# Cross-attention and a quantised feed-forward on one core: scores ahead of the up product in each tile's first slot

## The chip, the cores and the metric

The kernel runs on one core of a Trainium2 chip. A core has five engines with an instruction queue each, which run in order and meet only at semaphores: TensorE (PE in the profile; its weight loads stand apart as PEld), VectorE (DVE), ScalarE (ACT), GpSimd (POOL) and SyncE (SP), which issues nearly all DMA transfers. The metric is the device time of one execution in microseconds (us).

## The reference, cut to what matters

The input is 8 batches of 512 rows with 512 columns; the context has 120 rows per batch. A block of cross-attention with 16 heads of 32 columns is added to the input, then a feed-forward block whose weights are ternary and whose activations are rounded to 8 bits.

```python
def proj(x, w, bias): ...                       # 16 heads of 32
Q = proj(layernorm(x), wq, bq); K = proj(ctx, wk, bk); V = proj(ctx, wv, bv)
scores = jnp.einsum('bhqd,bhkd->bhqk', Q, K) / jnp.sqrt(32)
scores = jnp.where(mask == 0, 1e-09, scores)
attn = jax.nn.softmax(scores, axis=-1)
x = x + (attn @ V) @ wo + bo
...
# bitlinear(x, w, b) = act_quant(rmsnorm(x)) @ weight_quant(w).T + b
h = gelu(bitlinear(layernorm(x), w1, b1))       # 512 -> 2048
x = x + bitlinear(h, w2, b2)                    # 2048 -> 512
```

## The kernel before, in words

The rows are cut into 32 tiles of 128, four to a batch. Every tile passes through a software pipeline written out by hand: time is cut into 128 slots, four to a tile, and for each engine a function `slot(n)` lists, in program order, what that engine does in slot n. Different stages of several tiles stand in one slot. Nothing reorders the lists at run time, so what stands ahead of an instruction on its engine delays it.

What the slots hold, as far as it matters here:

- A softmax group is four of a tile's 16 heads, one group per slot. In a tile's first slot (n divisible by 4) `scores(k)` on PE computes the scores of all 16 heads: 16 products into the four PSUM banks `ps_s`, one bank per group. It waits until the exponentials of all four groups of the tile before have been read from these banks (`exp_done` at 4k; the last of them is group n-1).
- DVE masks and takes the maximum of group n in slot n (`softmax_max`, L831 and L834). ACT does the exponentials of group n-1 in slot n (`exps`, L693, four pairs of instructions), and then copies the transposed probabilities of group n-3 out of `ps_t` (L665). POOL scales the probabilities (L1114), PE transposes them (`turn_probs`, L466).
- From slot 14 on, each slot has one quarter of the up product of another tile: `ffn_up` on PE, four matmuls into the bank `ps_z` (L507), and `evac_up` on DVE, which copies and scales it into `hid` (L873). There is one `ps_z` bank, so `ffn_up` of slot n waits for `evac_up` of slot n-1 (`z_evac`).
- DVE's own order in a tile's first slot is fixed: `evac_down` (L892) and `oT_low` (L799) of other tiles, then `evac_up` (L873), then `softmax_max` (L831). In the other three slots `softmax_max` stands ahead of `evac_up`.
- ACT's GELU for a tile (L700) follows in the slot after its last up quarter, behind a table load; another table load stands ahead of the next exponentials.
- In a tile's fourth slot PE does attention times V (L478), in its second the output projection (L405). Projections and transposes for the next batch lie in between, in a pattern of 16 slots per batch (L405 with `wq`, L435, L412).

Slots 0, 4, 8 and 12 of a batch's 16 are first slots of a tile. Behind the up product and the scores, slots 0 and 4 go on with a transpose of the next batch's rows (L412), slots 8 and 12 with a q projection (L405). In the last batch, slots 112 to 127, there is neither.

Of the kernel before, what the change touches and what calls it, by code (L numbers as in the profile page):

```python
# [27 lines left out]
def xattn_bitffn_kernel(nc, x, ctx_in, mask, wq, bq, wk, bk, wv, bv, wo, bo, w1, b1, w2, b2, out):  # L28
# [5 lines left out]
    G = D // P  # L34
# [47 lines left out]
    def tile_at(n, first):  # L82
        k, r = divmod(n - first, FC)
        return k if r == 0 and 0 <= k < NT else None
# [42 lines left out]
    with ExitStack() as stack:  # L127
# [93 lines left out]
        def wait(eng, name, count):  # L221
            if count > 0:
                eng.wait_ge(s[name], count)
# [142 lines left out]
        def _(pe):  # L366
            def wait_free(use):

                kind, a, k = use
                if kind == "x":  # L370
                    wait(pe, "xT_low", KD * a + k + 1)
                elif kind == "k":
                    wait(pe, "keyT_ready", a + 1)
                elif kind == "c":
                    wait(pe, "turn_evac", YT_ACT[use] + 1)
                elif kind == "m":
                    wait(pe, "wT_dve", 2 * a + k // 2 + 1)
                else:
                    wait(pe, "y_evac", a + 1)
# [28 lines left out]
            def turn_xn(a, k):  # L408
                bank = turn_free(("x", a, k))
                wait(pe, "xn_ready", T * (a + 1))  # L410
                for t in range(T):
                    last = nc.tensor.transpose(bank[:, t * P:(t + 1) * P], xn[:, t, k * P:(k + 1) * P], ident[:])  # L412
                last.then_inc(s["turn_full"], 1)
# [17 lines left out]
            def project_ctx(a, what, w):  # L431
                bank = a_bank((what, a, 0))
                wait(pe, "turn_evac", YT_ACT[("c", a, 0)] + 1)
                for k in range(KD):
                    last = nc.tensor.matmul(bank[0:S2, :], ctxT[:, k], w[:, k], start=(k == 0), stop=(k == KD - 1))  # L435
                last.then_inc(s["a_full"], 1)

            def project_q(a, g):
                bank = a_bank(("q", a, g))
                if g == 0:  # L440
                    wait(pe, "xT_low", KD * (a + 1))
                for k in range(KD):
                    wh, wl = wq_h[:, k, g * P:(g + 1) * P], wq_l[:, k, g * P:(g + 1) * P]
                    last = product3(bank[:], k, ((wh, xnT_h[:, k]), (wh, xnT_l[:, k]), (wl, xnT_h[:, k])))
                last.then_inc(s["a_full"], 1)

            def scores(k):
                a = k // T
                wait(pe, "keyT_ready", a + 1)
                if k % T == 0:  # L450
                    wait(pe, "a_evac", AJ_ACT[("q", a, G - 1)] + 1)
                wait(pe, "exp_done", G * k)
                for g in range(G):
                    for i in range(HG):
                        rows = slice(i * HD, (i + 1) * HD)
                        last = nc.tensor.matmul(ps_s[i][:, g * S2:(g + 1) * S2], qT[rows, k % QR, g],  # L456
                                                keyT[rows, a % 2, g], start=True, stop=True)
                last.then_inc(s["sc_full"], 1)

            def turn_probs(n):  # L460
                if n == 0:
                    wait_free(YT[FIRST - 2])
                wait(pe, "p_evac", n)
                wait(pe, "prob_ready", n + 1)
                for g in range(G):
                    last = nc.tensor.transpose(ps_t[0:S2, g * P:(g + 1) * P], prob[:, n % 3, g * S2:(g + 1) * S2],  # L466
                                               ident[:])
                last.then_inc(s["p_full"], 1)

            def attend(k):  # L470
                a = k // T
                bank = a_bank(("o", k, 0))
                wait(pe, "v_ready", a + 1)
                wait(pe, "p_evac", G * k + HG)
                for g in range(G):
                    for i in range(HG):
                        h = g * HG + i
                        last = nc.tensor.matmul(bank[i * HD:(i + 1) * HD, g * P:(g + 1) * P],  # L478
                                                v_s[:, a % 2, h * HD:(h + 1) * HD], probT[0:S2, i, g],
                                                start=True, stop=True)  # L480
                last.then_inc(s["a_full"], 1)
# [10 lines left out]
            def ffn_up(k, c):  # L492
                j = FC * k + c
                if j == 0:
                    pe.wait_ge(s["wT_act"], 16)
                    pe.wait_ge(s["wT_dve"], 8)
                if j <= Z0:
                    wait(pe, "z_evac", j)
                else:
                    wait(pe, "z_evac", j - 2)  # L500
                    if j <= Z0 + 2:
                        pe.wait_ge(s["exp_done"], NU)
                if c == 0:
                    wait(pe, f"qxT{k % 3}_in", 16 * (k // 3 + 1))
                bank = z_bank(j)
                for i in range(KD):
                    last = nc.tensor.matmul(bank[:], q_xT[:, k % 3, i], w1T[:, i, c * CH:(c + 1) * CH],  # L507
                                            start=(i == 0), stop=(i == KD - 1))
                last.then_inc(s["z_full"], 1)
# [16 lines left out]
            def total_weights(m):  # L526
                pe.wait_ge(s["abs_act"], 2 * (m + 1))
                pe.wait_ge(s["abs_dve"], 2 * (m + 1))
                wait(pe, "wT_act", 8 * m)
                nc.tensor.matmul(ps_z[:, 0:4], ones, w_abs[:, m], start=True, stop=True).then_inc(s["w_sum"], 1)  # L530

            def turn_piece(j, quarters):
                p = TURN[j]
                if j % 2 == 0:
                    pe.wait_ge(s["w_ready_dve"], j // 2 + 1)
                else:
                    pe.wait_ge(s["w_ready_pool"], j // 2 + 1)
                for q in quarters:
                    if q % 2 == 0:
                        wait(pe, "wT_act", 2 * j + q // 2)  # L540
                        bank = ps_z
                    else:
                        wait_free(Y[Y_N[("m", j, q)] - 1])
                        bank = ps_y
                    for c in range(4):
                        col = c * D + q * P if p < 4 else (4 * q + c) * P
                        last = nc.tensor.transpose(bank[:, c * P:(c + 1) * P], piece_buf[p][:, col:col + P], ident[:])
                    last.then_inc(s["wT_full"], 1)

            def slot(n):  # L550
                if n >= LAG:
                    turn_probs(n - LAG)
                k = tile_at(n, ATT0)
                if k is not None:
                    attend(k)
                if n in TOTAL_AT:
                    total_weights(TOTAL_AT[n])
                if n in TURN_AT:
                    turn_piece(TURN_AT.index(n), (0, 1))
                if n >= UP0:  # L560
                    ffn_up((n - UP0) // FC, (n - UP0) % FC)
                if n % G == 0:
                    scores(n // G)
                if n in PROJ:
                    kind, b, g = PROJ[n]
                    if kind == "q":
                        project_q(b, g)
                    else:
                        if kind == "v" and b == 0:
                            pe.wait_ge(s["wv_in"], 16)  # L570
                        project_ctx(b, kind, wk_s if kind == "k" else wv_s)
                k = tile_at(n, WO0)
                if k is not None:
                    project_out(k)
                if n in TURN_AT:
                    turn_piece(TURN_AT.index(n), (2, 3))
                if n in TURNS:
                    kind, b, k = TURNS[n]
                    if kind == "x":
                        turn_xn(b, k)  # L580
                    elif kind == "c":
                        turn_ctx(b)
                    else:
                        turn_keys(b)
                for half in range(2):
                    k = tile_at(n, DOWN0 + half)
                    if k is not None:
                        ffn_down(k, half)
# [656 lines left out]
```

## Time and profile before

| | us |
|---|---|
| median of 3 runs | 743.72 |
| lowest and highest run | 740.01, 750.9 |
| profiled execution, time | 741.57 |
| its span, first to last instruction | 739.8 |

| engine | busy, share of the span |
|---|---|
| PE | 90% |
| DVE | 82% |
| ACT | 71% |
| POOL | 68% |

The span of the profiled execution is 1.8 us shorter than its time. A batch in the steady part takes about 78.6 us, 19.6 us per tile; two batches with their 32 slots lie between 298.6 and 456.1 us. A row of the timeline gives start, duration, engine, line, operation and tiles, and in square brackets the idle time of that engine just before it with what ended it, where there was any. The ends of matmuls are modelled, so that neighbouring matmuls seem to overlap; starts are the better measure.

### The profile page before, as it was taken

Reading aid. Unit: us, or ns where it says so; the run is one execution under the profiler, and the core shown is the slowest. Engines: PE = TensorE matmul, PEld = TensorE weight load, DVE = VectorE, ACT = ScalarE, POOL = GpSimd, SP = SyncE. Lnnn points to the kernel's source line nnn. Section 1 sums busy time; section 2 is a strip of 40 time slices with the busy share of each in tenths; the row PEclk is TensorE's granted clock in tenths of the full one; section 3 lists DMA queues with packets and bytes.
Section 4 is the critical chain, followed back from the end, with each engine's and each line's share of the span. In section 5 each row is a group of like instructions: output and inputs, shape, how many; then the busy total and the mean of one; then the engine's idle time right before and its main releaser. Section 6 shows DMA issues by size and latency. Waiting matters only on the chain.

```text
span 739.8 us, 13877 instructions
## 1 busy us (share of the span) xinstructions
PE 662.3 (90%) x4856; PEld 428.5 (58%) x4856; DVE 603.0 (82%) x1060; ACT 522.6 (71%) x1455; POOL 506.1 (68%) x645
## 2 busy tenths in 40 slices
PE   8755778989999999999999999999999998888885
PEld 6524566755666567656666666656665664554532
DVE  3397586689979898899888988989798888888783
ACT  2264536686888877886788678868888778887360
POOL 3036363766877787777977687768777668877764
PEclk9977979999999999999999999999999999999997
DMA  9943003034122433343334322351222333333244
GB/s 304 379 151 129 1 15 106 17 55 109 44 63 66 122 78 79 66 122 78 79 65 99 100 65 64 64 116 48 67 65 65 79 65 65 65 65 66 57 79 113
DMA packets 109204, 65.37 MB, mean 88 GB/s; under 512 B 90775, under 2 KB 90775, under 8 KB 108495
## 3 DMA queue, kind: packets, MB, share of 16 engines
q1 hardware_dynamic: 108079, 64.49, 34.9%
q8 instruction: 39, 0.64, 0.3%
q14 instruction: 30, 0.25, 0.1%
q10 hardware_dynamic: 1056, 0.00, 0.1%
HBM read 35.12 MB, written 8.39 MB: 59 GB/s over the span
## 4 chain that ended last, share of the span: by engine, by line
PE 39%; DVE 30%; ACT 11%; issue 7%; POOL 5%; DMA 5%; SPq 3%; DVEq 0%; POOLq 0%; ACTq 0%
PE ps_a L405 13%; PE ps_z L507 6%; PE ps_y L522 5%; PE ps_a L435 4%; DVE hs L880 4%; DVE yw L857 3%; DMA q_xT<-q_x 3%; DVE hid L873 3%; PE ps_a L478 3%; ACT prob L693 3%; PE ps_t L466 2%; POOL hid L1121 2%; POOL q_h L1128 2%; DVE yq L860 2%; DVE bn L817 2%
## 5 line engine op out<-in xcount | busy, mean ns | idle before, releaser
L1114 POOL TENSOR_TENSOR prob<-prob,pinv 128x480 f32<-128x480 f32 x128 | 126.5, 988 | 166.5 <-DVE pinv L839 166.4
L693 ACT ACTIVATE prob<-ps_s,nmax 128x120 f32<-128x120 f32 x512 | 180.5, 384 | 25.2 <-DVE nmax L834 24.9
L507 PE MATMUL ps_z<-w1T,q_xT 128*128 128x512 bf16 x476 | 123.1, 381 | 5.6 <-DMA q_xT<-q_x 5.5
L693 ACT ACTIVATION_READ_ACCUMULATOR prob<-ps_s,nmax 128x1 f32 x512 | 117.4, 229 | 0.0
L522 PE MATMUL ps_y<-w2T,q_hT 128*128 128x512 bf16 x480 | 113.2, 379 | 0.3 <-DMA q_hT<-xn 0.3
L873 DVE SCALAR_TENSOR_TENSOR hid<-ps_z,y_deq,b_row 128x512 f32<-128x512 f32 x119 | 88.6, 745 | 25.2 <-PE ps_z L507 25.1
L831 DVE COPY_PREDICATED_SCALAR ps_s<-hidden_key,masked_c 128x480 f32 x128 | 89.6, 700 | 18.0 <-PE ps_s L456 18.0
L466 PE MATMUL ps_t<-ident,prob 128*120 128x128 f32 x512 | 79.0, 277 | 12.8 <-ACT probT L665 10.2
L834 DVE TENSOR_REDUCE nmax<-ps_s 128x4 f32<-128x480 f32 x128 | 84.2, 658 | 4.4
L665 ACT COPY probT<-ps_t 120x512 f32<-120x512 f32 x128 | 79.5, 621 | 8.7 <-PE ps_t L466 8.6
L522 PEld LDWEIGHTS ps_y<-w2T,q_hT 128*128 128x128 bf16 x480 | 45.9, 98 | 61.1 <-issue 10.4
L466 PEld LDWEIGHTS ps_t<-ident,prob 128*120 128x120 f32 x512 | 60.1, 139 | 33.9 <-ACT probT L665 19.7
L672 ACT ACTIVATE qT<-ps_a,bq_col 128x512 f32<-128x512 f32 (+1 forms) x32 | 19.7, 616 | 75.6 <-PE ps_a L405 70.9
L880 DVE TENSOR_REDUCE hs<-hid 128x1 f32<-128x2048 f32 x32 | 72.8, 2276 | 0.0
L1121 POOL TENSOR_SCALAR hid<-hid,hs 128x2048 f32<-128x2048 f32 x31 | 61.1, 1972 | 13.5 <-DVE hs L886 7.1
L700 ACT ACTIVATE hid<-hid 128x2048 f32<-128x2048 f32 x32 | 61.2, 1913 | 11.3 <-DVE hid L873 11.0
L507 PEld LDWEIGHTS ps_z<-w1T,q_xT 128*128 128x128 bf16 x476 | 43.5, 98 | 43.5 <-issue 13.5
L1128 POOL TENSOR_SCALAR q_h<-hid 128x2048 bf16<-128x2048 f32 x30 | 58.0, 1933 | 2.6
L405 PE MATMUL ps_a<-xnT_h,wq_h 128*128 128x512 f32 x124 | 52.7, 425 | 7.8 <-DVE oT_l L799 3.9
L405 PE MATMUL ps_a<-wo_h,oT_h 128*128 128x512 f32 x128 | 56.9, 444 | 2.4 <-DVE oT_l L799 1.5
L708 ACT ACTIVATE q_h<-hid 128x2048 bf16<-128x2048 f32 x28 | 54.3, 1938 | 0.0
L405 PE MATMUL ps_a<-wo_l,oT_h 128*128 128x512 f32 x128 | 50.9, 398 | 0.0
(155 smaller groups left out, 1400.8 us busy)
## 6 DMA issues: line engine op xcount, KB each, us to landing
xn<-in_x_dram SPq DMA_DIRECT2D x8, 1024.0 KB, 5.8
x<-in_x_dram SPq DMA_DIRECT2D x32, 256.0 KB, 2.7
out_dram<-x SPq DMA_DIRECT2D x32, 256.0 KB, 3.4
hid<-in_L_ffn_w_dram SPq DMA_DIRECT2D x4, 1024.0 KB, 8.9
w2T<-in_L_ffn_w_dram SPq DMA_DIRECT2D x2, 1024.0 KB, 14.0
ctx_k<-in_ctx_dram SPq DMA_DIRECT2D x8, 240.0 KB, 3.7
ctx_k<-in_mask_Bx1xSxS_ik_dram SPq DMA_DIRECT2D x7, 240.0 KB, 2.9
wk_s<-in_L_xattn_wk_dram SPq DMA_DIRECT2D x1, 1024.0 KB, 8.8
```

The lines of the kernel that those rows point to most:

```text
L405: last = nc.tensor.matmul(bank, w, m, start=(k == 0 and i == 0), stop=(k == KD - 1 and i == 2))
L466: last = nc.tensor.transpose(ps_t[0:S2, g * P:(g + 1) * P], prob[:, n % 3, g * S2:(g + 1) * S2], ident[:])
L507: last = nc.tensor.matmul(bank[:], q_xT[:, k % 3, i], w1T[:, i, c * CH:(c + 1) * CH], start=(i == 0), stop=(i == KD - 1))
L522: last = nc.tensor.matmul(y_bank(k)[:], q_hT[:, k % 2, f], w2T[:, f], start=(f == 0), stop=(f == KF - 1))
L665: nc.scalar.copy(probT[0:S2, i], ps_t[0:S2, :].rearrange("p (g q) -> p g q", g=G)).then_inc(s["p_evac"], 1)
L693: last = nc.scalar.activation(prob[:, n % 3, g * S2:(g + 1) * S2], ps_s[n % HG][:, g * S2:(g + 1) * S2], ACT.Exp, bias=nmax[:, n % 4, g:g ...
L831: v.copy_predicated(sc, hidden_key[:, k // T % 2, k % T].unsqueeze(1).to_broadcast([P, G, S2]), masked_c[:].unsqueeze(2).to_broadcast([P, ...
L834: v.tensor_reduce(out=nmax[:, n % 4], in_=sc, op=ALU.max, axis=AX_X, negate=True).then_inc(s["sc_max"], 1)
L873: v.scalar_tensor_tensor(hid[:, k % 2, c * CH:(c + 1) * CH], z_bank(FC * k + c)[:], y_deq[:, k % 8:k % 8 + 1], b1_row[:, c * CH:(c + 1) * ...
L880: v.tensor_reduce(out=hs[:, 3, t:t + 1], in_=hid[:, k % 2], op=ALU.max, axis=AX_X, apply_absolute_value=True).then_inc(s["h_abs"], 1)
L1114: gp.tensor_tensor(pr, pr, pinv[:, n % 4].unsqueeze(2).to_broadcast([P, HG, S2]), ALU.mult).then_inc(s["prob_ready"], 1)
L1121: gp.tensor_scalar(hid[:, k % 2], hid[:, k % 2], hs[:, 5, t:t + 1], MAGIC, ALU.mult, ALU.add).then_inc(s["h_magic"], 1)
```

## The change: what it does, and the diff

In the list of PE, `scores` moves from behind `ffn_up` to ahead of it. Since scores are only in slots with n divisible by 4, only these slots change, and of them only those from slot 16 on, where there is an up product. No instruction is added or removed, and the lists of the other engines and their waits are as before.

```diff
                 if n in TURN_AT:
                     turn_piece(TURN_AT.index(n), (0, 1))
+                if n % G == 0:
+                    scores(n // G)
                 if n >= UP0:
                     ffn_up((n - UP0) // FC, (n - UP0) % FC)
-                if n % G == 0:
-                    scores(n // G)
                 if n in PROJ:
```

PE's queue around slot 64, a batch's slot 0. The first two rows are the end of the fourth slot of the tile before, the last row is the head of slot 65. Before the change:

```order
L507 MATMUL ps_z<-w1T,q_xT 128x512 x3
L522 MATMUL ps_y<-w2T,q_hT 128x512 x8
L466 MATMUL ps_t<-ident,prob 120x128 [waits prob_ready,p_evac]
L466 MATMUL ps_t<-ident,prob 120x128 x3
L507 MATMUL ps_z<-w1T,q_xT 128x512 [waits z_evac]
L507 MATMUL ps_z<-w1T,q_xT 128x512 x3
L456 MATMUL ps_s<-keyT,qT 128x120 [waits exp_done,keyT_ready]
L456 MATMUL ps_s<-keyT,qT 128x120 x15
L412 MATMUL ps_y<-ident,xn 128x128 [waits xn_ready,y_evac]
L412 MATMUL ps_y<-ident,xn 128x128 x3
L466 MATMUL ps_t<-ident,prob 120x128 [waits prob_ready,p_evac]
```

The same place with the change:

```order
L507 MATMUL ps_z<-w1T,q_xT 128x512 x3
L522 MATMUL ps_y<-w2T,q_hT 128x512 x8
L466 MATMUL ps_t<-ident,prob 120x128 [waits prob_ready,p_evac]
L466 MATMUL ps_t<-ident,prob 120x128 x3
L456 MATMUL ps_s<-keyT,qT 128x120 [waits exp_done,keyT_ready]
L456 MATMUL ps_s<-keyT,qT 128x120 x15
L507 MATMUL ps_z<-w1T,q_xT 128x512 [waits z_evac]
L507 MATMUL ps_z<-w1T,q_xT 128x512 x3
L412 MATMUL ps_y<-ident,xn 128x128 [waits xn_ready,y_evac]
L412 MATMUL ps_y<-ident,xn 128x128 x3
L466 MATMUL ps_t<-ident,prob 120x128 [waits prob_ready,p_evac]
```

The wait for `exp_done` now stands ahead of the up product's four matmuls.

DVE's queue in the same slot, equal before and with the change:

```order
L839 RECIPROCAL pinv<-psums 128x4 [waits exp_done]
L892 SCALAR_TENSOR_TENSOR x<-ps_y,h_deq,x 128x512 [waits y_full,hdeq_ready,x2b2_ready]
L799 TENSOR_TENSOR oT_l<-ps_a,oT_h 128x512 [waits a_evac]
L873 SCALAR_TENSOR_TENSOR hid<-ps_z,y_deq,b_row 128x512 [waits z_full]
L831 COPY_PREDICATED ps_s<-hidden_key,masked_c 128x480 [waits sc_full]
L834 TENSOR_REDUCE nmax<-ps_s 128x4 [waits sc_masked]
L839 RECIPROCAL pinv<-psums 128x4 [waits exp_done]
L831 COPY_PREDICATED ps_s<-hidden_key,masked_c 128x480 [waits sc_full]
```

Nothing moved here: L873, the copy of the up product, stands ahead of L831, the first reader of the scores.

## Rows read from the trace of the kernel before

**Rows 1.** The page, part 1: engine, busy us (share of the span) xinstructions.
```profile
PE 662.3 (90%) x4856; PEld 428.5 (58%) x4856; DVE 603.0 (82%) x1060; ACT 522.6 (71%) x1455; POOL 506.1 (68%) x645
```

**Rows 2.** Windows: busy us (instructions) of PE, PEld, DVE, ACT, POOL, then clock, DMA.
```profile
155.00:165.00 10.00, 7.91 (x61) 5.32 (x60) 8.43 (x16) 6.86 (x31) 9.27 (x12) 0.83 0.48 60
377.45:456.05 78.60, 76.75 (x585) 49.86 (x584) 69.29 (x128) 63.77 (x179) 60.74 (x80) 1.00 0.35 81
612.00:668.00 56.00, 46.24 (x417) 28.44 (x418) 50.08 (x92) 45.18 (x135) 45.47 (x58) 1.00 0.37 66
```

**Rows 3.** Timeline, slot 64: PE.
```profile
376.80 0.65 PE L466 MATMUL ps_t<-ident,prob 128*120 128x128 f32 x4 [0.21 <-ACT probT L665]
377.28 1.03 PE L507 MATMUL ps_z<-w1T,q_xT 128*128 128x512 bf16 x4
378.27 1.17 PE L456 MATMUL ps_s<-keyT,qT 32*128 32x120 f32 x32
379.37 0.66 PE L412 MATMUL ps_y<-ident,xn 128*128 128x128 f32 x4
```

**Rows 4.** Timeline, slot 64: ACT, a copy, and the last exponentials of the tile before.
```profile
376.07 0.67 ACT L665 COPY probT<-ps_t 120x512 f32<-120x512 f32 x1
...
377.81 0.31 ACT L693 ACTIVATION_READ_ACCUMULATOR prob<-ps_s,nmax 128x1 f32 x1
```

**Rows 5.** Timeline, slot 64: DVE.
```profile
379.17 0.74 DVE L873 SCALAR_TENSOR_TENSOR hid<-ps_z,y_deq,b_row 128x512 f32<-128x512 f32 x1
379.82 0.71 DVE L831 COPY_PREDICATED_SCALAR ps_s<-hidden_key,masked_c 128x480 f32 x1
```

**Rows 6.** Timeline, slot 67: PE's up product and DVE's copy of it.
```profile
392.79 1.04 PE L507 MATMUL ps_z<-w1T,q_xT 128*128 128x512 bf16 x4
393.86 0.75 DVE L873 SCALAR_TENSOR_TENSOR hid<-ps_z,y_deq,b_row 128x512 f32<-128x512 f32 x1 [0.81 <-PE ps_z L507]
```

**Rows 7.** Waits of ACT from 381.3 to 396.8: total us, times, longest.
```profile
ACT prob L693 <- DVE nmax L834: 0.6, 1, 0.6
```

**Rows 8.** Timeline, slot 68: ACT's last exponentials and DVE's copy.
```profile
395.99 0.30 ACT L693 ACTIVATION_READ_ACCUMULATOR prob<-ps_s,nmax 128x1 f32 x1
397.52 0.74 DVE L873 SCALAR_TENSOR_TENSOR hid<-ps_z,y_deq,b_row 128x512 f32<-128x512 f32 x1
```

**Rows 9.** Timeline, slot 72: ACT, PE and DVE.
```profile
414.11 0.23 ACT L693 ACTIVATION_READ_ACCUMULATOR prob<-ps_s,nmax 128x1 f32 x1
414.35 0.60 PE L466 MATMUL ps_t<-ident,prob 128*120 128x128 f32 x4
417.86 0.74 DVE L873 SCALAR_TENSOR_TENSOR hid<-ps_z,y_deq,b_row 128x512 f32<-128x512 f32 x1
```

**Rows 10.** Timeline, slot 20: ACT, PE and DVE.
```profile
158.99 0.30 ACT L693 ACTIVATION_READ_ACCUMULATOR prob<-ps_s,nmax 128x1 f32 x1
157.97 0.65 PE L466 MATMUL ps_t<-ident,prob 128*120 128x128 f32 x4 [2.09 <-ACT probT L665]
159.91 2.08 PE L456 MATMUL ps_s<-keyT,qT 32*128 32x120 f32 x32
162.05 0.72 DVE L831 COPY_PREDICATED_SCALAR ps_s<-hidden_key,masked_c 128x480 f32 x1 [1.29 <-PE ps_s L456]
```

**Rows 11.** Timeline, slot 108: ACT and PE.
```profile
592.85 0.31 ACT L693 ACTIVATION_READ_ACCUMULATOR prob<-ps_s,nmax 128x1 f32 x1
594.60 0.50 PE L405 MATMUL ps_a<-xnT_h,wq_h 128*128 128x512 f32 x1
```

**Rows 12.** Timeline, slot 112: ACT and DVE.
```profile
612.91 0.31 ACT L693 ACTIVATION_READ_ACCUMULATOR prob<-ps_s,nmax 128x1 f32 x1
614.28 0.74 DVE L873 SCALAR_TENSOR_TENSOR hid<-ps_z,y_deq,b_row 128x512 f32<-128x512 f32 x1
```

**Rows 13.** Timeline, slot 124: ACT and DVE.
```profile
664.96 0.29 ACT L693 ACTIVATION_READ_ACCUMULATOR prob<-ps_s,nmax 128x1 f32 x1
666.85 0.74 DVE L873 SCALAR_TENSOR_TENSOR hid<-ps_z,y_deq,b_row 128x512 f32<-128x512 f32 x1
```

## Prediction

> **What bounds the kernel now.** I read the page's part 1 first: PE is busy 90% of the span, DVE 82%, ACT 71% [rows 1]. That names no engine that is always the limit. The windows say more: in the batch from 377.45 to 456.05 us PE is idle for 78.60 - 76.75 = 1.85 us only, at full clock, and in the last batch for 56.00 - 46.24 = 9.76 us, also at full clock [rows 2]. So the steady part has hardly any room on PE, but the question is which wait ends last around the moved product, and that is read from the timeline of slot 64 on three engines.
>
> On PE the up product starts at 377.28, the scores at 378.27, the next step at 379.37 [rows 3]. So the up product takes 0.99 us there and the scores 1.10, from start to start. The scores need `exp_done` of the group before. On ACT that is the last accumulator read, which ends at 377.81 + 0.31 = 378.12 [rows 4]: 0.84 us after the start of the up product, and 0.15 us before the scores start. The reader is to see that the up product now fills exactly the time in which ACT finishes. PE does not wait for `exp_done` because it has this other work first. On DVE the copy of the up product starts at 379.17, after DVE's other work and without idle time before it, and the mask on the scores follows at 379.82 [rows 5]. The up product was ready about a microsecond earlier, so DVE, not PE, sets the pace here.
>
> **The change, part by part.** Nothing is added or removed; 16 score products and 4 up matmuls change places in the 28 first slots from 16 to 124. The list of PE now has the wait for `exp_done` ahead of both. Queued behind it on PE are the up product and all that follows; DVE waits for the up product with the scores' own reader behind that; ACT waits for DVE's maximum. The DMA queue is not moved past anything: SP waits for DVE and POOL results that precede the copy.
>
> *The new path in a slot.* From the end of ACT's last read to DVE's copy there are three steps. ACT's end to PE's start: ACT's copy ends at 376.07 + 0.67 = 376.74 and PE starts at 376.80, 0.06 [rows 3, 4]. The scores: 1.10. The up product up to DVE's start, where DVE was waiting for it: 393.86 - 392.79 = 1.07 [rows 6]. Together 2.23 us.
>
> *Slot 64* (a batch's slot 0): 378.12 + 2.23 = 380.35 against 379.17 [rows 5], so DVE is 1.18 us late. Who carries it on? The mask and maximum come right behind the copy, and the next exponentials on ACT already waited 0.6 us for that maximum, which is ACT's only wait from 381.3 to 396.8 us [rows 7]. ACT therefore starts 1.18 us late and works without a break up to the last exponentials of the tile. It has nothing in which the delay could be lost, although DVE has: it waits 0.81 us for PE at 393.86 [rows 6].
>
> *Slot 68* (slot 4): ACT's last read ends at 395.99 + 0.30 = 396.29, plus 2.23 is 398.52 against 397.52 [rows 8]: another 1.00 us, on top of the 1.18 that ACT brings along. PE comes earlier than ACT in both.
>
> *Slots 72 and 76* (8 and 12): no loss. In slot 72 ACT is done at 414.34, before PE's transposes that start at 414.35. The scores could start 0.48 us behind those (376.80 to 377.28 in [rows 3]), at 414.83, and 1.10 + 1.07 later DVE could copy, at 417.00, but it comes only at 417.86 [rows 9]. Slot 76 reads the same with less to spare. No gain either: DVE takes the up product first, so scores that are ready a microsecond sooner are read by nobody.
>
> So a batch loses 1.18 + 1.00 = 2.18 us. Five batches read like this (slots 32 to 107): 10.9 us. Around them:
>
> - Slot 16 reads like slot 68: 1.0.
> - Slot 20: PE has been idle 2.09 us before its transposes, and the scores take 2.08 us instead of 1.17; the mask waits 1.29 us for them [rows 3, 10]. The mean clock from 155 to 165 us is 0.83 [rows 2], so PE spends about a third of that at the lower of its two levels (1.2 GHz) and the rest at 2.4. ACT is done at 158.99 + 0.30 = 159.29; scores at 159.35, up product at 161.43 if still slow, copy at 162.50 at full clock and 163.57 at the lower one, mask 0.65 later [rows 5], against 162.05 [rows 10]: 1.1 to 2.2 late. I take 1.3, near the lower end, since the third of 10 us is over by about then.
> - Slot 108: ACT's end at 593.16, plus 0.06 and 1.10 and the 0.99 of the up product gives 595.31 for the projection, which started at 594.60 [rows 11]: 0.7.
> - The last batch, four slots: 613.22 + 2.23 against 614.28 is 1.17 [rows 12], 665.25 + 2.23 against 666.85 is 0.63 [rows 13]; four times their mean, 0.9, is 3.6.
>
> Sum: 1.0 + 1.3 + 10.9 + 0.7 + 3.6 = 17.5 us. The profiled execution took 741.57 us, so 759.1; that execution lies 2.2 us below the median of 743.72, from which it would be 761.2. I forecast **760**. Bounds: nothing at the least, if every added wait falls into idle time; at the most 1.18 in all 28 slots, 33 us, which slots 72 and 76 exclude. The own range of this sum is 13 to 21 us.
>
> *The clock.* The row shows that PE's clock was low after the 2.09 us of idle time [rows 10], and high in the last batch with 9.76 us of idle time spread over it [rows 2]. The change puts some 0.7 us of new idle time (376.80 + 0.48 to 378.18) ahead of the scores in each losing slot. The Trainium skill (TensorE: Matmul & The Clock Gate, Part 1) says that the slow clock is the default that an idle engine falls back to, and its closing table warns of idle gaps between bursts of matmuls. By that rule this change could cost more than its waits; by the rows at full clock the sum stands as it is. The trace agrees with the rule at slot 20 and does not show it in the last batch.
>
> **Rivals.**
>
> *The waits swallow it* (not slower). If ACT does not carry the delay, because its order leaves it time that the rows don't show, only PE's own delay remains: 0.06 + 1.10 + 0.99 after 378.12 is 380.27 against 379.37, 0.90 us a slot, 1.8 for the two of a batch, and PE has 1.85 us of idle time in it [rows 2]. Then the five batches cost nothing and slot 16 neither, and 1.3 + 0.7 + 3.6 = 5.6 us are left: 747. For it speak DVE's 0.81 us; against it that ACT has one wait in 15 us [rows 7]. It decides from the point where ACT has 1.18 us to spare between the maximum of a tile's first group and its last exponentials. Chance 0.18.
>
> *The clock falls too* (slower still). In the last batch, where PE already idles most, each of the four slots would run scores and up product at the lower clock: 2.17 us more each, 8.7 in all, so 768. For it speaks slot 20, against it the clock of 1.00 from 612 to 668 us. Chance 0.13.
>
> *The early scores are worth something* (faster). If DVE's mask did wait for scores in many slots, they would come a microsecond sooner. Only slot 20 shows such a wait, 1.29 us [rows 10], so the gain would be a microsecond or two: 740. Chance 0.04. That the change does nothing is excluded, since PE's printed order does move and PE's queue is in order.
>
> **How the numbers follow.** The sum has 0.62, the rivals 0.18, 0.13 and 0.04, and 0.03 is left for something else. 2% is 14.9 us, about what a measurement of this kernel can tell from no change. Of the sum's 13 to 21 us about four fifths lie above that: 0.50, with the clock's 0.13 and 0.01 of the rest 0.64 for slower; faster by 2% has 0.02; the other 0.34 is within 2%. The range goes from 749 to 767: it has the whole of the sum from either base and the upper part of the first rival and the lower of the second.
>
> **What would show it.** In the changed kernel's slot 64: scores 0.05 to 0.1 us after ACT's last read with PE idle some 0.7 us before them, and DVE's copy waiting for PE where it had no wait; slots of the kinds 0 and 4 with this wait, 8 and 12 without; a batch of about 80.8 us instead of 78.6; ACT's idle time before the first exponentials of a tile longer by the same 1.2. The forecast is wrong if a batch stays at 78.6 us although DVE waits (first rival), or if PE's clock in the last batch is below 1.00 (second).

## The result, and the profile after

| | before | with the change |
|---|---|---|
| median, us | 747.21 (4 runs) | 761.3 (4 runs) |
| lowest and highest run | 740.01, 750.9 | 760.62, 761.52 |
| profiled execution, time and span | 741.57, 739.8 | 760.62, 758.8 |

The ratio of the mean times is 1.0199 with a 95% interval of 1.0109 to 1.0289: slower beyond its interval, though whether by more or by less than 2% stays open. A fourth run of the kernel before, beside the changed one, lifted its median from 743.72 to 747.21; in three later measurements it was 740.65, 743.02 and 740.85. The two profiled executions differ by 19.0 us in span and are compared below. The forecast was 760, with 749 to 767 as its range.

The page of the changed kernel, its parts 1 and 4:

```profile
PE 665.5 (88%) x4856; PEld 428.4 (56%) x4856; DVE 604.2 (80%) x1060; ACT 522.2 (69%) x1455; POOL 505.4 (67%) x645
...
ACT 46%; PE 22%; DVE 19%; issue 9%; DMA 2%; POOL 1%; SPq 0%; ACTq 0%; DVEq 0%; POOLq 0%
```

Busy times are those of before within 3.2 us [rows 1]: the 19 us are nearly all waits. Of the chain that ended last, 46% now lies on ACT, where it was 11%.

The timeline of slot 64, ACT, PE and DVE, in the order of [rows 3 to 5]:

```profile
384.76 0.31 ACT L693 ACTIVATION_READ_ACCUMULATOR prob<-ps_s,nmax 128x1 f32 x1
...
385.21 1.17 PE L456 MATMUL ps_s<-keyT,qT 32*128 32x120 f32 x32 [0.82 <-ACT prob L693]
...
386.31 1.04 PE L507 MATMUL ps_z<-w1T,q_xT 128*128 128x512 bf16 x4
...
387.19 0.60 PE L412 MATMUL ps_y<-ident,xn 128*128 128x128 f32 x4
...
387.39 0.75 DVE L873 SCALAR_TENSOR_TENSOR hid<-ps_z,y_deq,b_row 128x512 f32<-128x512 f32 x1 [1.19 <-PE ps_z L507]
...
388.06 0.71 DVE L831 COPY_PREDICATED_SCALAR ps_s<-hidden_key,masked_c 128x480 f32 x1
```

PE, which had no wait here, now stands idle for 0.82 us and starts at 385.21, 0.14 us after ACT's read ends at 385.07, and DVE stands idle for 1.19 us where it had no wait. From ACT's end to DVE's copy it takes 387.39 - 385.07 = 2.32 us.

The chain of waits in the same place (start, us, what):

```profile
383.69 1.39 ACT prob L693 x8
385.08 0.14 issue
385.21 1.17 PE ps_s L456 x32
386.38 0.98 PE ps_z L507 x4
387.36 0.02 issue
387.39 0.03 DVE hid L873
387.42 0.64 issue
388.06 0.72 DVE ps_s L831
388.78 0.02 issue
388.80 0.67 DVE nmax L834
389.47 0.02 issue
389.50 1.48 ACT prob L693 x8
390.97 0.48 ACT probT L665
391.45 0.02 issue
391.47 1.05 ACT L700
...
402.64 0.49 ACT probT L665
403.13 1.39 ACT prob L693 x8
404.52 0.14 issue
404.65 1.17 PE ps_s L456 x32
```

From 389.50 to 404.52 the chain does not leave ACT, and at its end stands slot 68 with the same pattern again. ACT's wait for the maximum, at the head of that stretch, grew from 0.6 us [rows 7] to 1.1:

```profile
ACT prob L693 <- DVE nmax L834: 1.1, 1, 1.1
```

That growth is less than half of the delay, because another wait now takes up part of the same time, one that the prediction did not name: ACT's list has the copy of PE's transposes (L655) before the exponentials, and these transposes come later too. First before, then with the change:

```profile
380.06 0.59 ACT L655 CAST xnT_h<-ps_y 128x512 fp32r<-128x512 f32 x1 [1.46 <-PE ps_y L412]
```

```profile
387.82 0.58 ACT L655 CAST xnT_h<-ps_y 128x512 fp32r<-128x512 f32 x1 [2.28 <-PE ps_y L412]
```

Together ACT's idle time ahead of the tile's first exponentials grew by (2.28 - 1.46) + (1.1 - 0.6) = 1.3 us, where 1.2 was forecast. The maximum is still the later of the two: the exponentials start at 389.50, right behind it.

The window of the batch that starts with slot 64 (columns as in [rows 2]):

```profile
383.50:464.40 80.90, 77.10 (x584) 49.73 (x584) 70.07 (x128) 63.64 (x179) 60.65 (x80) 1.00 0.34 79
```

The batch takes some 80.9 us instead of 78.6, at full clock.

As the common measure of all kernels I take the start of DVE's mask on a tile's first group (L831). From slot 28 to slot 104 it takes 372.68 us before and 384.34 with the change: 11.66 more, or **2.33 us a batch** over five batches, each with one slot of kind 0 and one of kind 4. All per-batch numbers below are made like this, against the profiled execution of before. Between these slots the granted clock is 1.00 in the profiled execution of every kernel of this document, so they are free of the clock; spans and medians are not.

### The profile page after: what moved, and what is told of

It is laid out like the page before. It is cut to its first block, busy times and chain, and to the rows that moved or that the text cites. A ratio compares the mean times of both kernels' runs of the same rounds, so it can differ in the third digit from the quotient of the medians.

```text
span 758.8 us, 13877 instructions
## 1 busy us (share of the span) xinstructions
PE 665.5 (88%) x4856; PEld 428.4 (56%) x4856; DVE 604.2 (80%) x1060; ACT 522.2 (69%) x1455; POOL 505.4 (67%) x645
## 4 chain that ended last, share of the span: by engine, by line
ACT 46%; PE 22%; DVE 19%; issue 9%; DMA 2%; POOL 1%; SPq 0%; ACTq 0%; DVEq 0%; POOLq 0%
ACT prob L693 17%; PE ps_a L405 8%; ACT hid L700 6%; ACT q_h L708 5%; ACT probT L665 4%; PE ps_s L456 4%; PE ps_z L507 4%; ACT L693 4%; ACT L700 4%; DVE hs L880 2%; DVE hid L873 2%; DVE yw L857 2%; DVE ps_s L831 2%; DVE nmax L834 2%; PE ps_a L435 1%
## 5 line engine op out<-in xcount | busy, mean ns | idle before, releaser
L693 ACT ACTIVATE prob<-ps_s,nmax 128x120 f32<-128x120 f32 x512 | 180.0, 383 | 34.1 <-DVE nmax L834 33.8
L507 PE MATMUL ps_z<-w1T,q_xT 128*128 128x512 bf16 x476 | 125.4, 387 | 1.7 <-DVE hid L873 1.2
L873 DVE SCALAR_TENSOR_TENSOR hid<-ps_z,y_deq,b_row 128x512 f32<-128x512 f32 x119 | 88.6, 745 | 46.9 <-PE ps_z L507 46.4
L693 ACT ACTIVATION_READ_ACCUMULATOR prob<-ps_s,nmax 128x1 f32 x512 | 117.2, 229 | 0.0
L831 DVE COPY_PREDICATED_SCALAR ps_s<-hidden_key,masked_c 128x480 f32 x128 | 89.5, 699 | 16.2 <-PE ps_s L456 16.2
L665 ACT COPY probT<-ps_t 120x512 f32<-120x512 f32 x128 | 79.2, 619 | 11.1 <-PE ps_t L466 10.9
L700 ACT ACTIVATE hid<-hid 128x2048 f32<-128x2048 f32 x32 | 61.2, 1912 | 11.3 <-DVE hid L873 10.9
L507 PEld LDWEIGHTS ps_z<-w1T,q_xT 128*128 128x128 bf16 x476 | 40.6, 98 | 45.7 <-issue 9.0
L456 PE MATMUL ps_s<-keyT,qT 32*128 32x120 f32 x1024 | 39.5, 292 | 15.7 <-ACT prob L693 14.3
```

Of the source, the lines that this page charges most:

```text
L665: nc.scalar.copy(probT[0:S2, i], ps_t[0:S2, :].rearrange("p (g q) -> p g q", g=G)).then_inc(s["p_evac"], 1)
L693: last = nc.scalar.activation(prob[:, n % 3, g * S2:(g + 1) * S2], ps_s[n % HG][:, g * S2:(g + 1) * S2], ACT.Exp, bias=nmax[:, n % 4, g:g ...
L700: nc.scalar.activation(hid[:, k % 2], hid[:, k % 2], ACT.Gelu).then_inc(s["gelu_done"], 1)
L831: v.copy_predicated(sc, hidden_key[:, k // T % 2, k % T].unsqueeze(1).to_broadcast([P, G, S2]), masked_c[:].unsqueeze(2).to_broadcast([P, ...
L873: v.scalar_tensor_tensor(hid[:, k % 2, c * CH:(c + 1) * CH], z_bank(FC * k + c)[:], y_deq[:, k % 8:k % 8 + 1], b1_row[:, c * CH:(c + 1) * ...
```

## The experiments

**Only slots 8 and 12, and only slots 0 and 4.** The change is cut in two.

```diff
-                if n % G == 0:
+                if n % G == 0 and n % U in (8, 12):    # the other: (0, 4)
                     scores(n // G)
                 if n >= UP0:
                     ffn_up((n - UP0) // FC, (n - UP0) % FC)
+                if n % G == 0 and n % U not in (8, 12):
+                    scores(n // G)
```

> Scores ahead of the up product only in slots 8 and 12 of each batch's 16 (24, 28, ... 108, 120, 124); in slots 0 and 4 behind it as before. Theory (cost only where ACT's last exponentials end later than PE could start the scores): nothing up to slot 104, 0.3 to 0.7 us at 108, about 1.1 at 120 and 0.7 at 124, so 2 to 3 us above the kernel before, 742 of span. Rival (any scores ahead of the up product push DVE's copy back by their 1.1 us): 14 x 1.1 = 15 us, as much as the other half of the slots.

> The complement: scores ahead only in slots 0 and 4 of a batch (16, 20, 32, 36, ... 112, 116). Theory: nearly the whole loss, 16 us: 1.1 at slot 16, 2.0 at 20, five times 2.3, 1.2 and 1.1 in the last batch; span about 756. Rival (each first slot pays alike): about 10 us.

Measured: slots 8 and 12 alone 745.66 us, ratio 1.0053 (1.0015 to 1.0091), span 742.1, and -0.06 us a batch; slots 0 and 4 alone 759.3 us, ratio 1.0212 (1.0139 to 1.0286), span 752.6, and 2.34 us a batch. The halves are as different as the rows of ACT's end said: where ACT is done before PE gets there, scores ahead of the up product cost nothing. What the first half loses lies elsewhere: 1.5 us ahead of slot 12, where the kernels are alike, and 2.5 in the last batch, of which 1.4 were made up at the end. The second span is 3.4 us below what I expected, with the loss of the batches in full. Slot 20 added only 0.2 us in that execution, and the clock says why: PE had stood idle for 2.08 us ahead of its transposes as before, but the clock stayed at 1.00 from 158 to 166 us. It is also the lowest of that kernel's four executions; by the medians this half loses 18.7 us.

**The wait without the move.** PE's order is that of before, and the up product waits as well.

```diff
                 if n >= UP0:
+                    if n % G == 0:
+                        wait(pe, "exp_done", n)
                     ffn_up((n - UP0) // FC, (n - UP0) % FC)
```

> PE's order as before (up product, then scores), but the up product of a first slot also waits for exp_done. It parts the two costs: the wait put ahead of the up product, and the 1.1 us of scores put ahead of it. Theory, from the rows of before: the copy can start at 378.12 + 0.06 + 1.07 = 379.25 instead of 379.17, and the mask waits for the scores, 378.12 + 0.06 + 0.99 + 1.10 + 0.04 = 380.31 instead of 379.82, +0.5 in slot 64 and +0.3 in slot 68: 0.8 a batch, about 6 us in all, span 746. Rival (the whole loss is the wait, wherever the scores stand): 2.3 us a batch, span 757 to 759.

Measured: 752.6 us, ratio 1.0138 (1.007 to 1.0207), span 752.0, 1.00 us a batch. Slot 64, ACT, PE and DVE (the wait adds two lines to the source, L695, L875 and L833 are L693, L873 and L831):

```profile
382.24 0.31 ACT L695 ACTIVATION_READ_ACCUMULATOR prob<-ps_s,nmax 128x1 f32 x1
...
382.61 1.04 PE L507 MATMUL ps_z<-w1T,q_xT 128*128 128x512 bf16 x4 [0.73 <-ACT prob L695]
...
383.58 1.17 PE L456 MATMUL ps_s<-keyT,qT 32*128 32x120 f32 x32
...
383.69 0.75 DVE L875 SCALAR_TENSOR_TENSOR hid<-ps_z,y_deq,b_row 128x512 f32<-128x512 f32 x1
...
384.88 0.72 DVE L833 COPY_PREDICATED_SCALAR ps_s<-hidden_key,masked_c 128x480 f32 x1 [0.45 <-PE ps_s L456]
```

The wait is nearly as long as in the change (0.73 us), but the up product comes first behind it and DVE's copy is not idle before it; the mask then waits 0.45 us. So the same wait costs 1.0 us a batch in this order and 2.33 in the other. The span is 6 us above what I expected, and the batches (1.0 instead of 0.8) explain only 1 of it. Outside them 7.2 us were lost where my total left 2: 0.9 ahead of slot 12, where the kernels are alike, 1.5 between slots 12 and 28, 3.4 in the last batch and 1.4 behind it. In the last batch 1.85 us came in slot 120 alone, next to a stretch of low clock (a mean of 0.72 from 650 to 656 us); I did not take the others apart.

**DVE follows PE's order.** On top of the change, DVE's mask and maximum stand ahead of its copy in first slots from 16 on.

```diff
+                if n % G == 0 and n >= UP0:
+                    softmax_max(n)
                 if n >= UP0:
                     evac_up((n - UP0) // FC, (n - UP0) % FC)
                 ...
-                if n % G == 0:
+                if n % G == 0 and n < UP0:
                     softmax_max(n)
```

> PE as in the change, and DVE follows it: in first slots from 16 on the mask and maximum of the scores stand ahead of the copy of the up product. Theory (ACT carries the delay, and only the maximum feeds ACT): in slot 64 the scores are there at 378.18 + 1.10 + 0.04 = 379.32, so the mask starts at 379.32 instead of 379.82 and ACT starts its exponentials 0.5 us earlier than before; the copy comes 1.4 us later and with it the next up product (z_evac), which PE pays with about 1 us where it is not idle. Expected between 733 and 748, near the kernel before, and in any case over 10 us faster than the change. Rival (PE or DVE carries the delay): no better than the change, 757 to 760, since PE waits as long and the copy is later still.

Measured: 751.17 us, ratio 1.0113 (1.0049 to 1.0177), span 749.2, 1.08 us a batch. Faster than the change by 10 us, slower than before, and just outside what I expected. Slot 64, by ACT, PE, DVE:

```profile
381.33 0.31 ACT L693 ACTIVATION_READ_ACCUMULATOR prob<-ps_s,nmax 128x1 f32 x1
...
383.08 0.72 DVE L831 COPY_PREDICATED_SCALAR ps_s<-hidden_key,masked_c 128x480 f32 x1 [0.32 <-PE ps_s L456]
...
383.76 0.60 PE L412 MATMUL ps_y<-ident,xn 128*128 128x128 f32 x4
...
384.39 0.58 ACT L655 CAST xnT_h<-ps_y 128x512 fp32r<-128x512 f32 x1 [2.28 <-PE ps_y L412]
...
384.88 0.37 ACT L693 ACTIVATE prob<-ps_s,nmax 128x120 f32<-128x120 f32 x1
...
385.21 1.04 PE L507 MATMUL ps_z<-w1T,q_xT 128*128 128x512 bf16 x4 [0.42 <-DVE hid L873]
```

The mask does start sooner after ACT's end (1.44 us instead of 1.70 before), but ACT gains nothing by it: its list has the copy of PE's transposes (L655) ahead of the exponentials, and these transposes are late behind scores and up product. I had left that wait out. And the late copy makes PE wait 0.42 us.

**ACT without its table loads.** GELU is replaced by an identity in both kernels; its function is left out.

```diff
-                nc.scalar.activation(hid[:, k % 2], hid[:, k % 2], ACT.Gelu).then_inc(s["gelu_done"], 1)
+                nc.scalar.activation(hid[:, k % 2], hid[:, k % 2], ACT.Identity).then_inc(s["gelu_done"], 1)
```

> The kernel before with the GELU replaced by an identity, which is in the same table as the exponentials: the computation leaves out the GELU's function, and ACT loses its two table loads of 1.28 us per tile. It is the base for the next run. ACT has 2.56 us a tile to spare, but DVE and PE set most of the chain of before: 730 to 740 us.

> The same edit on the changed kernel (GELU left out, no table loads). Theory (the loss is ACT's late exponentials, carried from one first slot to the next by an ACT without slack): with 2.56 us a tile taken out of ACT's chain the exponentials are done before PE needs them, and this run lies within 6 us of the run without loads and scores behind, at most 0.8 us a batch. Rival (the loss is the 1.1 us of scores put ahead of the up product, on PE and DVE, whatever ACT does): 2.3 us a batch and 17 to 19 us in all, as between the two kernels themselves.

Measured: scores behind 733.05 us, ahead 739.98; spans 730.7 and 736.9, 6.2 us apart instead of 19.0; -1.18 and -0.13 us a batch, so 1.05 apart instead of 2.33. With 2.56 us a tile taken out of ACT's chain, more than half of the loss a batch is gone. The two waits of PE for ACT in a batch fell from 1.6 us to 0.5 (windows 383.5 to 464.4 of the change and 376 to 455 of this run):

```profile
PE ps_s L456 <- ACT prob L693: 1.6, 2, 0.8
```

```profile
PE ps_s L456 <- ACT prob L693: 0.5, 2, 0.3
```

They did not go to zero, and the difference is a little over what I allowed (0.8 a batch). How much of the 1.05 that are left still hangs on ACT, these two kernels do not say.

**Ahead, but without the wait.** Two attempts. In the first, the fourth bank's products were computed for the second bank instead, so that the third group's exponentials are enough.

```diff
-                wait(pe, "exp_done", G * k)
+                wait(pe, "exp_done", G * k - 1 if k >= 4 else G * k)
                 for g in range(G):
                     for i in range(HG):
+                        if k >= 4 and i == 3:
+                            i = 1
```

> The changed order without its wait: from slot 16 on the four products meant for the fourth bank are computed for the second bank instead (same count and size, so the fourth group's scores are left out and stay those of an old tile), and the scores then need only the exponentials of the third group, which are long done. Theory: in slot 64 the scores start at 377.28 and the copy can start 1.10 + 1.07 later, at 379.45, against 379.17: 0.3 us; in slot 68 395.82 + 2.17 = 397.99 against 397.52: 0.5. So 0.8 us a batch at most, about 6 us in all, 741 to 747 of span, against 758.8 with the wait. Rival (the order costs, not the wait): above 755.

Measured: 770.68 us, ratio 1.0359 (1.0302 to 1.0415), span 769.1. This looked like a refutation and is a fault of the experiment. PE has no wait for ACT in front of the scores any more, but they take longer:

```profile
389.09 2.05 PE L458 MATMUL ps_s<-keyT,qT 32*128 32x120 f32 x32
```

The four products of one round of the inner loop use four different groups of 32 rows (`rows`) and write four different banks; with two of the four in the same row group, and so in the same bank, 16 products took 2.05 us instead of 1.17 [rows 3], both at full clock. Row group and bank changed together, so this run does not say which of them costs. The wait of 0.8 us was exchanged for 0.9 us of work.

In the second attempt the fourth group's products are left out from slot 16 on (`continue` in place of `i = 1`), in three kernels: ahead without the wait, ahead with it, and behind.

> The run before this kind was spoilt by its substitute: products that shared a row group took 2.05 us instead of 1.17. Now from slot 16 on the fourth group's products are left out (12 scores instead of 16, some 0.83 us), scores stand ahead of the up product, and they need only the third group's exponentials. Theory (the wait is the cost): slot 64 copy at 377.28 + 0.83 + 1.07 = 379.18 against 379.17, slot 68 395.82 + 1.90 = 397.72 against 397.52, so 0 to 0.2 us a batch and 1 to 3 us above the 12 products behind. Rival (the scores' time ahead of the up product costs even without the wait): 0.8 us a slot, above 1.5 a batch, 10 us or more.

> The same 12 products ahead, with the wait for all four groups' exponentials as in the change. Theory: slot 64 378.12 + 0.06 + 0.83 + 1.07 = 380.08 against 379.17, 0.9; slot 68 0.7; 1.65 a batch and 11 to 14 us above the 12 products behind. Rival (the order, not the wait): the same as without the wait.

> The base of the two: 12 products from slot 16 on, behind the up product as in the kernel before. DVE sets the pace in the first slots, so 0.27 us less of PE moves little: 736 to 740 of span.

Measured, in this order: 749.45 us, 762.7 and 745.69, ratios to the kernel before 1.0109 (1.0071 to 1.0146), 1.0268 (1.0142 to 1.0394) and 1.0051 (1.002 to 1.0081). Spans 745.9, 762.0, 744.5. A batch costs 0.62 us ahead without the wait and 2.32 with it. So, with the same work in the same order, the wait alone makes 1.7 of 2.3 us. In both the loss is larger than I expected (0 to 0.2 and 1.65 a batch), and for one reason. I had taken 0.83 us for 12 products, but they take as long as 16, as the row of the kernel with the wait shows,

```profile
387.76 1.16 PE L458 MATMUL ps_s<-keyT,qT 32*128 32x120 f32 x24 [0.82 <-ACT prob L695]
```

and with 1.10 us of scores the rows of before give 0.3 + 0.5 = 0.8 us a batch, as I had worked out for the first attempt. The base with 12 products behind is itself 4.7 us longer than before although it does less (I expected no more than 740 of span). Its trace shows where: 1.4 us came between slots 20 and 24, where the mean clock from 162 to 168 us is 0.67 against 0.98 before; and 2.0 between slots 48 and 52, where an up product waited 0.78 us for a transfer (`q_xT`) that was in time before and one DVE instruction (L857 of before) took 2.09 us instead of 0.98. In the other batches it runs as before, within 0.12 us.

**An attempt at a faster kernel.** From the kernel before, with DVE's residue L799 behind the maximum in slots 0 and 4.

```diff
+                k = tile_at(n, LOW0)
+                if k is not None and n >= U and n % U in (0, 4):
+                    oT_low(k)
```

(and the two places ahead leave it out in these slots.)

> An attempt at a version faster than both: the kernel before, with DVE's residue of the attention output (L799, 0.66 us) behind the maximum in slots 0 and 4 of a batch instead of ahead of the copy. The mask then waits for the scores alone: 379.41 instead of 379.82 in slot 64, so ACT starts 0.4 us earlier; the output projection on PE, which needs this residue, starts at about 381.45 instead of 380.97. If ACT carries the chain, up to 0.4 us for each of 16 slots, 6 us faster, 734; if PE does, up to 6 us slower, 746. I expect 736 to 740.

Measured: 741.95 us against 743.02, ratio 0.9968 (0.9937 to 1.0), span 738.6. A batch got 0.08 us longer. The span is within what I expected, but that is no change that this measurement can tell: no version here beats the kernel before.

## Why the prediction was right, point by point

The forecast, 760, and the mechanism held. Start of the mask, by slot, with the change against before:

| term | forecast, us | measured, us |
|---|---|---|
| slot 16 | 1.0 | 1.1 |
| slot 20 | 1.3 | 2.0 |
| five batches, slots 0 and 4 | 10.9 | 11.7 |
| slots 24 and 28 | 0 | -0.1 |
| slot 108 | 0.7 | 0.3 |
| last batch, four slots | 3.6 | 5.1 |
| sum | 17.5 | 20.0 |

The span differs by 19.0, since the changed kernel's execution was 0.7 us ahead before slot 16, and made up 0.3 us at the end. So it is partly luck that the forecast came so close: the terms were 2.5 us short, and 1.0 of that was hidden in stretches for which the sum has no term (ahead of slot 16 and behind slot 124). By medians the difference is 14.1 us against the four runs of before beside it, and 20.65 against the lowest of the three later medians.

*The new path.* I put 2.23 us from ACT's last read to DVE's copy; it is 2.32. The step that was mis-sized is ACT's end to PE's start: 0.06 us by the row of a copy and the transposes behind it, and 0.14 with the scores. It is not the accumulator read that makes the difference: in the kernel with the wait alone the up product started 0.06 us after such a read (382.24 + 0.31 = 382.55, and 382.61). It goes with the matmuls that wait, and why is not shown. 0.09 in each of ten slots is 0.9, against the 0.8 us that the five batches came out above the forecast. (The 0.7 us of new idle time that I gave for PE does not fit its own bracket, which makes 0.90; it was 0.82.)

*Who carries it.* With the change the chain lies on ACT from the first exponentials of a tile to the last. Shortening ACT's chain takes away 1.3 of 2.33 us a batch. The first rival (the waits swallow it, 747) has failed: DVE's idle time behind slot 64 swallowed nothing, since ACT was late by the same amount. What I left out, ACT's wait for PE's transposes (L655), does no more in slot 64 than take up time in which ACT would have waited for the maximum. But not the whole loss is PE's wait for ACT: with 12 products the order by itself costs 0.62 us a batch.

*Slots 8 and 12* cost nothing up to slot 104, by themselves and within the change. In slot 72, ACT ended at 423.41 + 0.23 = 423.64, ahead of PE's transposes at 423.66:

```profile
423.41 0.23 ACT L693 ACTIVATION_READ_ACCUMULATOR prob<-ps_s,nmax 128x1 f32 x1
```

*Slot 20.* Between my bounds of 1.1 and 2.2 us I chose 1.3, since I took the low clock to be over by the time of the up product. It was not:

```profile
159.81 2.08 PE L456 MATMUL ps_s<-keyT,qT 32*128 32x120 f32 x32 [0.36 <-ACT prob L693]
...
161.82 1.89 PE L507 MATMUL ps_z<-w1T,q_xT 128*128 128x512 bf16 x4
```

The granted clock by windows, before (first) and with the change:

```profile
158.00:160.00 2.00, 2.00 (x12) 0.89 (x12) 1.83 (x6) 1.77 (x9) 2.00 (x2) 0.71 0.00 0
...
162.00:164.00 2.00, 2.00 (x13) 1.61 (x14) 1.91 (x4) 1.08 (x4) 1.64 (x6) 0.94 1.29 57
164.00:166.00 2.00, 2.00 (x11) 1.59 (x10) 1.97 (x4) 1.98 (x8) 1.75 (x4) 1.00 1.11 219
```

```profile
158.00:160.00 2.00, 1.29 (x8) 0.92 (x12) 1.90 (x6) 2.00 (x10) 1.91 (x2) 0.54 0.00 0
...
162.00:164.00 2.00, 2.00 (x7) 1.03 (x6) 0.25 (x1) 0.00 (x0) 1.63 (x5) 0.50 1.13 210
164.00:166.00 2.00, 2.00 (x12) 1.61 (x11) 1.97 (x5) 0.73 (x2) 0.26 (x2) 0.75 0.95 80
```

From 160 to 162 us both have 0.50. A window of 2 us at a mean of 0.54 holds 2 x (1 - 0.54) / 0.5 = 1.8 us at the lower level, 1.2 GHz; added up, that is 3.4 us before and 6.8 with the change, where PE had been idle another 0.36 us for ACT. The up product took 1.89 us there instead of 1.04. That the change made the clock stay low is not shown: in the kernel with 12 products behind, whose order is that of before, it was low for 6.8 us too (0.79 from 158 to 160 us, 0.50 from 160 to 166), and with scores ahead in slots 0 and 4 alone it did not fall.

*The clock rival* (768) came true in part, and the sign that I had set for it, a clock below 1.00 in the last batch, did appear. It cost far less than the rival's 8.7 us, since up to slot 124 the clock fell once and not at all four slots. It fell after PE had been idle for 2.90 us:

```profile
659.11 0.65 PE L466 MATMUL ps_t<-ident,prob 128*120 128x128 f32 x4 [2.90 <-ACT probT L665]
659.69 1.77 PE L478 MATMUL ps_a<-probT,v_s 120*32 120x128 f32 x32
661.39 1.89 PE L507 MATMUL ps_z<-w1T,q_xT 128*128 128x512 bf16 x4
```

The window from 658 to 664 us has a mean clock of 0.72, the six windows from 640 to 654 have 1.00; and 650 to 668 of before had idle times of up to 1.6 us in front of the same transposes, at full clock. Slot 120, which follows, lost 1.84 us, where the other three slots of that batch lost 1.1 on average. The Trainium skill (TensorE: Matmul & The Clock Gate, Part 1 and closing table) warns of idle gaps between bursts of matmuls. The trace agrees with that at 659.11, but not every such gap did it: PE had stood idle for 2.77 us ahead of its transposes at 640.63 and for 2.94 us ahead of those at 678.30, and the clock stayed at 1.00. Nor is it shown that the change brought the fall: two kernels with the scores behind had one there as well, with a mean of 0.72 from 662 to 668 us (12 products behind) and of 0.57 from 660 to 664 (L799 behind the maximum). Behind slot 127 it fell once more (0.72 from 696 to 702 us, after 2.82 us of idle time), but in the last 33 us of the change its mean was 0.95, and 0.84 in the last 34 of before; there the two executions differ the other way.

The sum is 20.0 where 17.5 was forecast: 0.8 for the latency, 0.7 for slot 20, 1.5 in the last batch (by my estimate some 0.8 of it the clock, 1.84 less 1.1, and 0.4 the latency), less 0.4 at slot 108, to the rounding.

## What to carry to other kernels

On an engine with an in-order queue, look up for each wait what work stands behind it and whether the next engine needs that work: here a wait of 0.8 us with the up product behind it and 1.1 us of scores in between cost 2.33 us per two slots, the same wait with the up product first 1.00, and the same order without the wait 0.62 (in a kernel with 12 of the 16 products, which took as long). Idle time of one engine does not swallow a delay if another engine on the way round has none: find the engine whose row of waits is short in the stretch between two such places, and count the delay at full size there.

## What the runs showed of the hardware

- Twelve score products in three row groups took 1.16 us and sixteen in four 1.17, but sixteen in three, with one group and its bank used twice in each round, 2.05. Here the time goes by how often the busiest row group or bank is used, not by the number of products; which of the two it is was not tried.
- From the end of an accumulator read on ACT to the scores that waited for it passed 0.14 us, to an up product that waited for such a read 0.06, and from the end of a plain copy to PE's transposes 0.06. The difference goes with the matmuls that wait, not with what ACT did.
- After an idle time of PE of 2.08 or 2.09 us ahead of slot 20 the clock stayed at 1.00 in one kernel's execution, and was at the lower level for 3.4 us in another and for 6.8 in a third; after 2.90 us it fell, after 2.94 us in the same execution it did not. Two kernels are best compared over a stretch in which both have full clock, as slots 28 to 104 are here; a single slot next to such a gap tells little of the change.
